# A mixture-of-experts attention kernel: the value tiles kept in two buffers by even and odd steps, and two steps per loop round on TensorE and VectorE

## What is computed

```python
def _moe_attn(x, Wq, Wk, Wv, Wo, Wsel_v, Wsel_o):
    q = _rope(jnp.einsum('bsd,hdp->bhsp', x, Wq))
    k = _rope(jnp.einsum('bsd,hdp->bhsp', x, Wk))
    gv = _gate(x, Wsel_v)                       # top 2 of 8 experts, sigmoid
    v = jnp.einsum('bsd,bhse,hedp->bhsp', x, gv, Wv)
    att = jax.nn.softmax(jnp.einsum('bhsp,bhtp->bhst', q, k) / np.sqrt(P), axis=-1)
    o = jnp.einsum('bhst,bhtp->bhsp', att, v)
    go = _gate(x, Wsel_o)
    return jnp.einsum('bhsp,bhse,hepd->bsd', o, go, Wo)
```

## Time and profile before

| | us |
|---|---|
| time, median of 3 runs | 3324.17 (3323.59 to 3324.88) |
| the profiled execution's own time | 3322.09 |
| span of its trace | 3320.0 |
| PE busy | 3194.8 (96%) |
| DVE busy | 2459.3 (74%) |
| ACT busy | 2006.3 (60%) |
| POOL busy | 1578.1 (48%) |

### The profile page before, as it was taken

One profiled execution on the slowest core, in us unless ns is written; L12 is line 12 of the kernel. 1 busy time (PEld: TensorE's weight loads), 2 busy tenths in 40 slices (PEclk: granted clock), 3 DMA queues, 4 the chain that ended last, 5 costly groups with the idle time before them and its releaser, 6 DMA issues.

```text
span 3320.0 us, 67575 instructions
## 1 busy us (share of the span) xinstructions
PE 3194.8 (96%) x19648; PEld 2394.5 (72%) x19648; DVE 2459.3 (74%) x4686; ACT 2006.3 (60%) x4635; POOL 1578.1 (48%) x1295
## 2 busy tenths in 40 slices
PE   4899999999999999999999999999999999998997
PEld 3677777777777777777777777777777777776887
DVE  7677777777777777777777777777777777776896
ACT  4566665666666666666666666666666666565443
POOL 5243554335543554435543454435544444435777
PEclk8999999999999999999999999999999999999999
DMA  5232332333233332333333332333323333333222
GB/s 191 72 89 70 104 94 75 85 92 99 70 86 77 100 98 67 89 88 99 81 75 85 93 99 70 86 95 95 86 67 89 88 99 82 74 83 107 85 84 77
DMA packets 116199, 294.21 MB, mean 89 GB/s; under 512 B 33856, under 2 KB 54592, under 8 KB 99776
## 3 DMA queue, kind: packets, MB, share of 16 engines
q1 hardware_dynamic: 116160, 293.73, 33.8%
HBM read 261.69 MB, written 31.98 MB: 88 GB/s over the span
## 4 chain that ended last, share of the span: by engine, by line
PE 71%; DVE 19%; issue 6%; ACT 1%; POOL 1%; DVEq 0%; DMA 0%; SPq 0%; POOLq 0%; ACTq 0%
PE bank L760 24%; PE bank L903 14%; PE bank L818 9%; PE bank L876 7%; PE bank L775 5%; DVE nmax L1350 4%; PE bank L847 2%; DVE vm L1371 2%; PE bank L780 2%; PE bank L888 2%; DVE vm L1414 2%; DVE uf L1458 2%; PE bank L1011 2%; PE bank L856 2%; DVE vm L1396 1%
## 5 line engine op out<-in xcount | busy, mean ns | idle before, releaser
L616 POOL TENSOR_TENSOR u_l<-uf,u_h 128x512 fp32r<-128x512 f32 x508 | 683.5, 1356 | 716.0 <-ACT u_h L1183 716.0
L1350 DVE TENSOR_REDUCE nmax<-bank 128x1 f32<-128x512 f32 (+3 forms) x1024 | 552.5, 580 | 374.2 <-PE bank L775 368.5
L760 PE MATMUL bank<-wv_h,xx 128*128 128x512 f32 x2048 | 745.6, 410 | 11.2 <-DVE vm L1371 5.9
L1093 ACT ACTIVATE probs<-bank,nmax 128x512 f32<-128x512 f32 (+3 forms) x1024 | 590.7, 610 | 258.5 <-DVE nmax L1350 258.5
L1183 ACT ACTIVATE u_h<-uf 128x512 fp32r<-128x512 f32 x508 | 320.5, 631 | 652.5 <-DVE uf L1458 504.5
L760 PEld LDWEIGHTS bank<-wv_h,xx 128*128 128x128 f32 x2048 | 386.7, 189 | 192.0 <-issue 69.3
L611 POOL TENSOR_TENSOR v_sb<-v_next,zero_hb 128x512 f32<-128x512 f32 x64 | 74.6, 1166 | 876.0 <-PE bank L876 876.0
L903 PE MATMUL bank<-u_h,wo_h 128*128 128x512 f32 x1016 | 429.8, 423 | 32.7 <-issue 27.2
L818 PE MATMUL bank<-ident_sb,probs 128*128 128x128 f32 x3328 | 451.1, 274 | 2.3 <-ACT pt_e L1113 1.2
L818 PEld LDWEIGHTS bank<-ident_sb,probs 128*128 128x128 f32 x3328 | 386.6, 141 | 69.1 <-issue 13.3
L1458 DVE TENSOR_TENSOR uf<-oo,go 128x512 f32<-128x512 f32 x508 | 420.3, 837 | 2.6 <-POOL u_l L616 0.4
(11 more groups left out here) (202 smaller groups left out, 5623.7 us busy)
## 6 DMA issues: line engine op xcount, KB each, us to landing
go<-go_d SPq DMA_DIRECT2D x256, 512.0 KB, 6.5
xx<-xs_d SPq DMA_DIRECT2D x126, 512.0 KB, 4.9
oo<-scale_d SPq DMA_DIRECT2D x128, 128.0 KB, 2.9
a_d<-a_out SPq DMA_DIRECT2D x128, 128.0 KB, 2.3
st<-in_wv SPq DMA_DIRECT2D x16, 512.0 KB, 5.7
st<-in_wo SPq DMA_DIRECT2D x16, 512.0 KB, 7.4
pt_c<-in_x SPq DMA_DIRECT2D x12, 512.0 KB, 6.7
go_d<-go_turned SPq DMA_DIRECT2D x256, 8.0 KB
```

Source lines behind the costliest of these rows:

```text
L616: nc.gpsimd.tensor_tensor(low, full, high.bitcast(f32), ALU.subtract).then_inc(ul_done, 1)
L760: last = nc.tensor.matmul(out, lhs, rhs, start=n == 1, stop=n == 3 * len(chunks))
L1093: nc.scalar.activation(probs[:, s % 2, j, 0:w], sbank[j][:, 0:w], ACT.Exp, bias=nmax[:, 2 * s + j:2 * s + j + 1], **kw).then_inc(exp_done, 1)
L1350: nc.vector.tensor_reduce(nmax[:, 2 * s + j:2 * s + j + 1], sbank[j][:, 0:w], AX.X, ALU.max, negate=True).then_inc(nmax_ready, 1)
```

## The change

`v_next` and the copy go away. `v_sb` gets a leading dimension of two. DVE's summing instruction of `V` writes straight into `v_sb[:, odd]`, and PE's `AT` reads `v_sb[:, odd]`. Which half is meant must be known when the program is built, so PE and DVE have two steps in their loop body (`INNER` with `odd` 0 and with `odd` 1), and their loops run 31 rounds. ACT, POOL and SP keep their loops. `AT` waits for `v_ready` in place of `vc_ready`, and the wait of `V 0` for `vc_ready` is gone. The two halves together take the room that `v_next` and `v_sb` took.

```diff
-POOL_FILL = [[("VC", 0)],
+POOL_FILL = [[],
...
-        v_next = sb("v_next", [NP, TT, 2, P])
-        v_sb = sb("v_sb", [NP, TT, 2, P])
+        v_sb = sb("v_sb", [NP, 2, TT, 2, P])
...
-                    if name == "VC":
-                        if kind != FIRST:
-                            pool.wait_ge(w_full, w_at(kind, it, ("AT", 0))[2] + 1)
-                        pool.wait_ge(v_ready, it * 8 + 8)
-                        nc.gpsimd.tensor_tensor(v_sb[:].rearrange("q t j c -> q (t j c)"), v_next[:].rearrange("q t j c -> q (t j c)"), zero_hb[:], ALU.add).then_inc(vc_ready, 1)
-                    elif name == "UL":
+                    if name == "UL":
...
-                    pe.wait_ge(vc_ready, of + 1)
+                    pe.wait_ge(v_ready, of * 8 + 8)
...
-                                mm = nc.tensor.matmul(o[j * P + c:j * P + c + STRIP, :], v_sb[:, k, j, c:c + STRIP], pt_e[:, j, k, :], start=k == 0, stop=k == TT - 1)
+                                mm = nc.tensor.matmul(o[j * P + c:j * P + c + STRIP, :], v_sb[:, odd if kind != TAIL else 1, k, j, c:c + STRIP], pt_e[:, j, k, :], start=k == 0, stop=k == TT - 1)
...
-            with pe.Fori(1, PAIRS - 1) as it:
-                body(INNER, it)
+            with pe.Fori(1, PAIRS - 1, 2) as it:
+                body(INNER, it, 0)
+                body(INNER, it + 1, 1)
...
-                    if i == 0:
-                        if kind != PRO:
-                            dve.wait_ge(vc_ready, n)
...
-                    nc.vector.tensor_reduce(v_next[:, t, j, :], m, AX.X, ALU.add).then_inc(v_ready, 1)
+                    nc.vector.tensor_reduce(v_sb[:, odd, t, j, :], m, AX.X, ALU.add).then_inc(v_ready, 1)
...
-            body(FIRST, 0)
-            with dve.Fori(1, PAIRS - 1) as it:
-                body(INNER, it)
+            body(FIRST, 0, 1)
+            with dve.Fori(1, PAIRS - 1, 2) as it:
+                body(INNER, it, 0)
+                body(INNER, it + 1, 1)
```

More of the change, by code:

```diff
@@ L306, in build @@
         v_ready = sem("v_ready")
-        vc_ready = sem("vc_ready")
         va_ready = sem("va_ready")
@@ L794, in turn_y, with body @@
                     mm.then_inc(c_full[f"y{i}"], 1)
-            def body(kind, it):
+            def body(kind, it, odd=0):
                 n = it + 1 if kind != PRO else 0
```

## The result

| | us |
|---|---|
| time after, median of 3 runs | 3289.81 (3288.92 to 3291.09) |
| time before, median of 3 runs | 3324.17 (3323.59 to 3324.88) |
| ratio | 0.990, 95% interval 0.988 to 0.991 |
| profiled execution after, own time | 3291.09 |

What follows compares the result with a forecast made beforehand. PE, busy for 96% of the span, was taken as the bound, so gains must come from its gaps. The copy's 20.8 us plus the seam's 7.8 made 28.6, from 3324.17 to 3295.6 us; range 3284 to 3312.

Steps and rivals of the forecast that it cites:

- The copy: POOL's copy keeps DVE's `U 0` from finishing; without it each step gets 0.34 us shorter, taken as 0.335 x 62 = 20.8.
- The road of the delay: From `U 0` through `UH 0`, `UL 0`, `UL 1` and DVE's L1396 to PE's `V 3` and `J 4`, handed on one to one.
- still collides, by less: DVE's L1396 in `CH 1` (L1387 after) would still wait for POOL's `UL 1`, ending at about 1021.37 us.
- the 0.48 us named among the signs: Sign of being right: DVE's L1396 in `CH 1` takes about 0.48 us, where it took 0.83.
- `J 4` still waits, since 0.62 > 0.34: PE's `J 4`, 0.62 us late for POOL's `UL 4`, comes 0.34 earlier and stays about 0.6 late.
- `V 3` comes up: PE's `V 3`, held 0.26 us by DVE, comes up to 0.37 us earlier.
- The loop's seam: PE's branch between steps costs 0.27 us; one seam of two goes, 0.25 x 31 = 7.8 us, bounds 0 and 8.4.
- the expected 1.18: PE's time between steps without the branch: 0.52 us for the seam within a step plus 0.66 for six transposes, against 1.45.
- The race: POOL's `UL 4` always starts ahead of DVE's `U 5`: 0.18 x 62 = 11.2 us more gained, 3284.4; chance 0.08.
- The forecast of 45.9 and 46.15 in turn: Sign of being right: `ON` every 46.1 us on the mean, steps alternately about 46.15 and 45.9 us.
- The median: The 28.6 us taken off the profiled span, 3320.0 to 3291.4, was carried over to the median, 3324.17 to 3295.6.
- The loop that doesn't fit: PE's 1284-instruction loop is refetched each round: one to three 1.2 us stalls, 37 to 112 us, about 3370; chance 0.15.

Runs made afterwards that it cites:

- the two-step loop alone: The kernel before, copy kept, with only PE's loop at two steps a round and DVE's loop as before: 3314.16 us, ratio 0.996.
- the kernel with `UL 4` well ahead: The kernel after, with `UL 4` moved ahead of `RP 1` in POOL's table: 3251.91 us, ratio 0.979.
- the copy put elsewhere: The kernel after plus an idle 128x512 POOL copy, first in the step without the wait for `AT`, so it runs earlier: 3294.64 us, ratio 0.991.

## Why the prediction was right

**The copy (0.335 us a step, 20.8 us).** Right in place and in size. Putting the copy back cost 0.32 and 0.34 a step and 22.1 us in the loop; moving it to ACT saved 0.30 in the median step. The road of the delay is the predicted one: `U 0` ends 0.33 earlier, `UL 1` 0.34, L1387 is down to 0.48, the end of `V 1`'s gate product (it frees the bank for `V 3`) comes 0.33 earlier and `J 4` 0.33. L1387 stopped colliding altogether, where "still collides, by less" was forecast; the 0.48 us named among the signs was right.

**`J 4` still waits, since 0.62 > 0.34.** Right: 0.60 in the rows above. **`V 3` comes up.** Right, and it no longer waits.

**The loop's seam (0.25 x 31 = 7.8, at most 8.4).** Right in its mechanism and too small: 1.46 - 1.08 = 0.38 in the rows of one step, 0.34 in the median of the two-step loop alone, so 10.5 to 11.8 us. The step that failed is the one from the seam within a step. The prediction took two transposes and four bf16 matmuls from the earlier trace rows, 0.52 us, and added six transposes. Two of the four matmuls there (L780) are 256 wide and take until 0.12 us to the next; between two steps they are 128 wide, and all four start 0.06 apart. From the first of the four to the next projection it is 0.31 us there (1022.33 to 1022.64) and 0.20 between two steps (below). So the expected 1.18 should have been 1.07, and the seam without a branch takes 1.08. The bound of 0.27 came out of the same comparison, so the measured value lies outside it. First the seam within a step of the kernel before, then the one between two steps after:

```profile
1022.33 0.27 PE L780 MATMUL bank<-stackT 96*128 96x256 bf16 x1
1022.45 0.22 PE L781 MATMUL bank<-mask_sb,ident_hb 128*128 128x128 bf16 x1
```

```profile
1001.23 0.22 PE L773 MATMUL bank<-stackT 96*128 96x128 bf16 x1
1001.29 0.22 PE L774 MATMUL bank<-mask_sb,ident_hb 128*128 128x128 bf16 x1
```

**The race.** A chance of 0.08 was given to its always falling POOL's way, with the argument that both engines move by the same amount. It fell that way in 10 of the 30 odd steps and in none of the even ones; before it was 1 of 61. In such a step `UL 4` takes 1.29 (from 1025.79), and `J 4` is 0.05 us late only:

```profile
1026.90 0.40 PE L896 MATMUL bank<-u_h,wo_l 128*128 128x512 f32 x1
1027.18 0.47 PE L896 MATMUL bank<-u_h,wo_h 128*128 128x512 f32 x1
```

Those steps are 46.0 us instead of 46.12, so the race brought some 1 us of the 33. That part is luck. `J 4` gains 0.55 and the step a fifth of that, since the time is taken back later in it. DVE's `U 5` and PE ahead of `V 5` in the same step:

```profile
1025.79 1.84 DVE L1449 TENSOR_TENSOR uf<-oo,go 128x512 f32<-128x512 f32 x1
```

```profile
1036.01 0.50 PE L753 MATMUL bank<-wv_h,xx 128*128 128x512 f32 x1 [0.20 <-DVE q_l L1423]
```

Now `U 5` is the one that is held, 1.84 us instead of 0.68, and `U 6` after it, 1.68 instead of 0.93. PE waits for DVE's `q_l` ahead of `V 5`, by 0.38 us more than in the other steps. In the kernel with `UL 4` well ahead, `U 5` takes 1.34 and this wait isn't there, so the same gain at `J 4` arrives whole. That the race is worth 0.18 a step was taken from the one step of before.

**The account of the loop.** Against 46.48 the even steps are 0.69 shorter (31 of them: 21.3 us) and the odd ones 0.40 (30 of them: 11.9), 33.2 together. Of this the copy is 0.335 x 61 = 20.4, the seam 31 x 0.34 = 10.5, the race 1, and 1.3 are left. DVE's busy time tells the same: `U 0` lost 20 us over the run and L1387 (128 of them) 21, and the race gave 11 back in `U 5` and 7 in `U 6`; together 23, and DVE's busy time fell by 23.8. The forecast of 45.9 and 46.15 in turn is 45.79 and 46.11; the difference is the seam's.

**The median.** It moved by 34.4 us and the profiled execution by 31.0, because that one is the slowest of the three after, while the profiled one of before is below all three of those before. Carrying the profile's sum over to the median, as the prediction did, can be off by such an amount.

**The loop that doesn't fit.** It does fit: one fetch, no branch of over 0.24 us. The chance of 0.15 could not be decided from the trace of before. But its price can be measured now, and it was far too low: 1.2 to 3.6 us a round, from the time that a fetch takes once it runs. Where it does happen it is 9.5 to 9.6. The number of fetches was right (one, at times two, in a standstill); what the price left out is the time until the fetch starts (3.6 to 6.5 us where there is one), some 1.5 us behind it, and the half clock after it. The branch goes back 30 times in 31 rounds, so this would have been about 285 us, not 37 to 112: the case should have been priced at some 3580 us.

## What to carry to other kernels

A small instruction of GpSimd can cost its collision with VectorE at one place and next to nothing at another (22.1 and 3.8 us here): compare the durations of the neighbour's instructions with their ordinary ones before asking what the copy itself blocks, since moving it to a third engine or another time may give most of what removing it gives. A loop of the chip can be unrolled by two for about a third of a us a round on TensorE, as long as its instructions are held; measure that with the queue of instruction fetches, since the step over the edge cost 9.5 us a round here, twenty-eight times the gain. And after a change look again for what is late now: the wait left at `J 4` was worth more than the whole change, and one word in a table removed it, while the next word made another engine late.

## What the runs showed of the hardware

- A VectorE product of two operands in SBUF doesn't finish while a GpSimd copy that began clearly before it is at work: `U 0` grew by 0.33 beside a copy of 1.16 us and by 1.07 beside one of 1.89 us, and `U 0` and `U 1` ended 1.15 and 1.16 us behind the copy. An instruction with one operand in PSUM didn't grow (1.29 for two, beside the copy put elsewhere). Where the two engines start within 0.01 us of each other (`U 5` and `UL 4`), either can win, and the other takes 1.83 or 1.84 us instead of 1.29 or 0.68.
- A TensorE loop of 645 or of 1284 instructions is held (none and one fetch between its first branch and its last); one of 1925 or 2564 is fetched in every round (171 fetches in 19 rounds and 167 in 14). The edge is somewhere between 1284 and 1925.
- A branch back to code that is no longer held stands for 6.4 to 8.9 us on TensorE, one to held code for 0.21 to 0.24 us in the kernels before and after (0.08 where the loop ends), and the whole seam around that one costs 0.34 to 0.38.
- In the standstill looked at (6.23 us) TensorE's granted clock fell from 1.00 to 0.50. Work came back at 1283.87 us, the clock at 1288.
